# Cross-attention denominators from sums over four steps, joined by an accumulating DMA, in the first batch of a decoder layer

## What is computed

```python
q = (x1 @ wq.T).reshape(b, n, 16, 32).transpose(0, 2, 1, 3)
k = (x2 @ wk.T).reshape(b, m, 16, 32).transpose(0, 2, 1, 3)
v = (x2 @ wv.T).reshape(b, m, 16, 32).transpose(0, 2, 1, 3)
dots = einsum('bhnd,bhmd->bhnm', q, k) * 32 ** -0.5
attn = softmax(dots, axis=-1)
out = einsum('bhnm,bhmd->bhnd', attn, v)       # then @ wo.T + bo, added to x1, layer norm
```

## Time and profile before

| | before |
|---|---|
| three runs | 2017.34, 2019.51, 2024.68 us |
| the profiled execution | 2017.9 us |
| its span, first to last instruction | 2016.1 us |
| PE busy | 1919.1 us (95%) |
| DVE, ACT, POOL busy | 1221.2, 882.5, 793.8 us |
| mean granted TensorE clock | 0.982 of full speed |
| DMA | 211.04 MB moved, 105 GB/s over the span |

### The profile page before, as it was taken

How to read it: one execution, slowest core, us unless ns; L and a number is a source line. 1 busy time by engine, 2 the same in 40 slices (tenths; PEclk the granted TensorE clock), 3 DMA queues, 4 the chain that set the end, 5 groups by cost and what they waited for, 6 DMA issues and landing times.

```text
span 2016.1 us, 26457 instructions
## 1 busy us (share of the span) xinstructions
PE 1919.1 (95%) x10152; PEld 1268.9 (63%) x10152; DVE 1221.2 (61%) x2279; ACT 882.5 (44%) x1587; POOL 793.8 (39%) x705
## 2 busy tenths in 40 slices
PE   6999999989999999999999999999969999999992
PEld 5876665667655555555444545544438999888991
DVE  5565543237677777777778779768654444444433
ACT  3212322222365666666556556546724443333431
POOL 3002200000177777777667657656012222322112
PEclk9999999999999999999999999999979999999996
DMA  6102433574533031312425334422234454444316
GB/s 247 42 1 99 155 107 131 184 220 126 161 96 85 17 76 47 95 43 59 100 65 131 75 93 113 121 48 74 79 111 137 126 138 125 112 136 101 104 22 187
DMA packets 119070, 211.04 MB, mean 105 GB/s; under 512 B 10608, under 2 KB 28672, under 8 KB 118864
## 3 DMA queue, kind: packets, MB, share of 16 engines
q1 hardware_dynamic: 108416, 185.39, 31.2%
q0 software_dynamic: 9440, 21.86, 5.6%
q10 hardware_dynamic: 1088, 2.10, 0.3%
HBM read 147.15 MB, written 62.42 MB: 104 GB/s over the span
## 4 chain that ended last, share of the span: by engine, by line
PE 85%; DVE 10%; DMA 2%; ACT 1%; issue 1%; SPq 0%; POOL 0%; ACTq 0%; POOLq 0%; DVEq 0%
PE banks L1070 36%; PE banks L1236 11%; PE banks L1325 11%; PE banks L1206 10%; PE banks L1225 9%; DVE max L1499 7%; PE banks L1254 5%; PE banks L1076 2%; DMA k_parts<-out_lo 1%; DMA wv_raw<-in_wv_t 1%; DVE stats_y L1707 0%; PE banks L1144 0%; DVE src_lo L1369 0%; DVE wq_lo L1375 0%; ACT src_hi L1754 0%
## 5 line engine op out<-in xcount | busy, mean ns | idle before, releaser
L1499 DVE TENSOR_REDUCE max<-banks 128x1 f32<-128x512 f32 x1024 | 627.6, 683 | 163.3 <-PE banks L1206 162.3
L1969 POOL TENSOR_TENSOR probs_sum<-probs_sum,probs_add 128x512 f32<-128x512 f32 x464 | 581.9, 1285 | 299.8 <-PE banks L1236 299.8
L1206 PE MATMUL banks<-k_stack,q_stack 98*128 98x512 f32 x1024 | 427.8, 425 | 3.7 <-DVE max L1499 2.7
L1847 ACT ACTIVATE probs_sum<-banks 128x512 f32<-128x512 f32 x512 | 264.6, 604 | 296.6 <-PE banks L1225 296.1
L1225 PE MATMUL banks<-q_stack,k_stack 98*128 98x512 f32 x1024 | 377.0, 398 | 2.0 <-ACT probs_sum L1847 2.0
L1206 PEld LDWEIGHTS banks<-k_stack,q_stack 98*128 98x128 f32 x1024 | 192.1, 188 | 190.8 <-issue 82.7
L1847 ACT ACTIVATE probs_add<-banks 128x512 f32<-128x512 f32 x512 | 272.6, 613 | 0.0
L1225 PEld LDWEIGHTS banks<-q_stack,k_stack 98*128 98x128 f32 x1024 | 191.9, 188 | 61.8 <-ACT probs_sum L1847 10.3
L2011 POOL DMA_INDIRECT y_rows<-eo,tok x40 | 81.5, 2037 | 216.4 <-DVE eo L1700 168.9
L1236 PE MATMUL banks<-probs_sum,v_grp 128*32 128x512 f32 x1024 | 139.9, 607 | 0.0
L1687 DVE TENSOR_TENSOR hid_lo<-hid,hid_hi 128x640 fp32r<-128x640 f32 x64 | 52.8, 826 | 140.6 <-ACT hid_hi L1912 140.6
(11 more groups left out here) (233 smaller groups left out, 2785.2 us busy)
## 6 DMA issues: line engine op xcount, KB each, us to landing
k_stack<-k_parts SPq DMA_DIRECT2D x144, 256.0 KB, 4.8
w_raw<-in_L_ffn_w SPq DMA_DIRECT2D x16, 2048.0 KB, 9.7
q_stack<-q_parts SPq DMA_DIRECT2D x48, 256.0 KB
v_grp<-v_rows SPq DMA_DIRECT2D x48, 256.0 KB, 3.1
raw<-in_ctx_t SPq DMA_DIRECT2D x8, 1024.0 KB, 6.7
k_parts<-out_hi SPq DMA_DIRECT2D x32, 256.0 KB, 2.5
k_parts<-out_lo SPq DMA_DIRECT2D x32, 256.0 KB, 2.9
v_rows<-pre SPq DMA_DIRECT2D x32, 256.0 KB, 2.3
```

What stands on the lines that cost most here:

```text
L1206: nc.tensor.matmul(out, queries_of(t)[:, j, tile_of(k)], keys_of(t)[0:STK + SHIFT, j, mc * HALF:(mc + 1) * HALF], start=True, stop=True) \
L1499: V.reduce_max(max4[:, tiles_of(t), :, :][:, k, j, mc:mc + 1], bank(bank_of["max", t, mc, k, j]), AX.X) \
L1847: S.activation(probs_of(t, s)[:, j, :], bank(bank_of["score", t, s, j]), ACT.Exp, scale=SCALE) \
L1969: done = G.tensor_tensor(a[:, j, :], a[:, j, :], b[:, j, :], ALU.add)
```

## The change

In turns 0 to 7, except the last four steps of turn 7, four steps share one denominator (`by_fours`): 31 fours. Their even steps no longer share one set of tiles: step 0 of a four writes `probs_sum` (three tiles, round again after twelve steps), step 2 writes a new set `probs_mid` (two tiles, eight steps), the odd steps write `probs_add` as before. POOL adds both pairs as before, and then issues one DMA that accumulates the tile of `probs_mid` (128 x 2048, 1 MB) into that of `probs_sum`, from SBUF to SBUF (`add_four`). It stands on POOL just ahead of the next pair's addition. The denominator of the four is put in the list three blocks after the four's second pair instead of one. ACT waits for the DMA before it writes the `probs_mid` tile again. The second batch keeps pairs, but its even steps use the two sets too.

The memory for this comes from `y_nat`, now one tile instead of two (the second half's rows are fetched only when the first half's are stored), from moving `earlier`, `kv`, `kv_part` and `att_t`, and from a `dynamic_dma_scratch_size` of 8192. `num_c` gets two buffers, and the inversions of a turn start at another block. The three pieces of a key chunk and the four of a query stack become single entries of the list: in the first batch one of each kind per block, in the second three key pieces.

```diff
+        def by_fours(t, s):
+            return t * MT + s < B * NG * MT - FOUR
+
+        def four_of(t, s):
+            return (t * MT + s) // FOUR % len(probs[0])
...
-                if s == 1:
+                if s == (3 if by_fours(t, 0) else 1):
                     take_bank(("den", t), DEN)
                 do("den", t, s)
                 if s == MT - 1:
                     do("copy_den", t)
                     divisions.extend((t, q) for q in range(PIECES))
+                    divisions_from[0] = clock
...
         def loads_after_scores(t, s):
             stay = stay_of[t]
-            if t == last_of[stay] and s % HT == HT - 1:
-                load_k(stay + 2, s // HT)
-            if s == MT - 1:
-                load_q(t + PLACES)
+            if t == last_of[stay] and s % HT == HT - 1 and stay + 2 < len(stays):
+                key_loads.extend((stay + 2, s // HT, i) for i in range(PARTS))
+            for _ in range(1 if t < B * NG else PARTS):
+                if key_loads:
+                    do("load_k", *key_loads.pop(0))
+            if s == MT - 1 and t + PLACES < len(turns):
+                query_loads.extend((t + PLACES, i) for i in range(PARTS + 1))
+            if query_loads:
+                do("load_q", *query_loads.pop(0))
...
                 if not end:
+                    while fours:
+                        do("add_four", *fours.pop())
                     do("add_pair", turn, s + 1)
-                    pending.append((clock + 1, turn, s + 1))
-                invert(4 if turn == LAST else (0, 2, 2)[s // 2] if s < 6 else 1, 1)
-                if g == NG - 2 and s == 2:
+                    if not by_fours(turn, s):
+                        pending.append((clock + 1, turn, s + 1))
+                    elif s % FOUR == 2:
+                        fours.append((turn, s + 1))
+                        pending.append((clock + 3, turn, s + 1))
+                invert(4 if turn == LAST else 0 if clock == divisions_from[0] else
+                       2 if clock < divisions_from[0] + 3 or turn == B * NG - 1 else 1, 1)
+                if g == NG - 2 and s == 2 and (b or not h):
                     start_side(fetch_rows(b, h))
...
+            place, every = PLACE_OF[s % FOUR]
+            return probs[place][(t * MT + s) // every % len(probs[place])]
...
                     act.wait_ge(*num_summed[t0, s0])
-                    if s0 % 2 == 0:
-                        act.wait_ge(*den_summed[t0, s0 + 1])
+                    if s0 % FOUR == 0:
+                        act.wait_ge(*den_summed[t0, s0 + (3 if by_fours(t0, s0) else 1)])
+                    elif s0 % FOUR == 2:
+                        act.wait_ge(*fours_added[four_of(t0, s0)][t0, s0 + 1] if by_fours(t0, s0)
+                                    else den_summed[t0, s0 + 1])
...
+            def add_four(t, s):
+                pool.wait_ge(*pair_added[t, s])
+                G.dma_start(probs_of(t, s - 3)[:, :, :], probs_of(t, s - 1)[:, :, :], accum_op=ALU.add) \
+                    .then_inc(fours_added[four_of(t, s)].sem, 16)
```

More of the change, by code:

```diff
@@ L182, in program @@
         v_grp = put("v_grp", [P, MT, P])
-        probs = [[put(f"probs_{name}{i}", [P, HG, HALF]) for i in range(n)] for name, n in (("sum", 3), ("add", 3))]
+        probs = [[put(f"probs_{name}{i}", [P, HG, HALF]) for i in range(n)]
+                 for name, n in (("sum", 3), ("add", 3), ("mid", 2))]
         shift_rows = put("shift_rows", [SHIFT * HG * HT, P], F32R)
-        context_base = put.at = put.at + 1024
+        context_base = put.at
         q_stack.append(put("q_stack2", [P, HG, HALF], F32R))
@@ L192, in program @@
         xwo = put("xwo_t", [P, NC, D])
-        y_nat = [put(f"y_nat{i}", [P, HT, D]) for i in range(NH)]
+        y_nat = put("y_nat", [P, HT, D])
         log_parts_at = put.at
@@ L196, in program @@
         hot_col = put("hot_col", [P, TOPK, HT, 2, COLS])
-        num_c = put("num_c", [P, HALF])
+        num_c = [put(f"num_c{i}", [P, HALF]) for i in range(2)]
         den_c = put("den_c", [P, HALF])
@@ L239, in program @@
         bq_col = put("bq_col", [P, NG])
+        kv, kv_part = put("kv", [P, NG, P + HG]), put("kv_part", [P, NG, P + 1])
+        att_t = put("att_t", [P, NG, P])
         den = put("den", [P, H])
@@ L637, in load_k @@
             if stay < len(stays):
-                do("load_k", stay, c)
+                for i in range(PARTS):
+                    do("load_k", stay, c, i)
         def load_q(t):
             if t < len(turns):
-                do("load_q", t)
+                for i in range(PARTS + 1):
+                    do("load_q", t, i)
         def load_v(stay, c):
@@ L742, in side @@
             return True
-        divisions, pending, later = [], [], []
+        divisions, pending, later, fours, divisions_from = [], [], [], [], [0]
         clock = 0
@@ L754, in divide @@
                 elif g == NG - 1 and t < LAST:
+                    if not b and h:
+                        start_side(fetch_rows(b, h))
                     start_side(rows_of(b, h))
@@ L1052, in probs_before @@
         def probs_before(t, s):
-            earlier_step = t * MT + s - 2 * len(probs[s % 2])
+            place, every = PLACE_OF[s % FOUR]
+            earlier_step = t * MT + s - every * len(probs[place])
             return divmod(earlier_step, MT) if earlier_step >= 0 else None
@@ L1157, in fold @@
                 pe.wait_ge(*const_in[()])
-                by_column_groups(out, [(router_pad[:, c, :], y_nat[0][:, c, :]) for c in range(NC)]) \
+                by_column_groups(out, [(router_pad[:, c, :], y_nat[:, c, :]) for c in range(NC)]) \
                     .then_inc(folds_summed.sem, 1)
@@ L1241, in denominators_of @@
             def denominators_of(t, s):
-                if s == 1:
+                first = s - 3 if by_fours(t, s) else s - 1
+                if first == 0:
                     free_bank("den", t)
-                tiles = [probs_of(t, s - 1)]
+                tiles = [probs_of(t, first)]
                 if t == LAST and s == MT - 1:
@@ L1254, in denominators_of @@
                         done = nc.tensor.matmul(bank(DEN)[j * DH:(j + 1) * DH, :], ones[:, 0:DH], tile[:, j, :],
-                                                start=s == 1, stop=s == MT - 1 and tile is tiles[-1])
+                                                start=first == 0, stop=s == MT - 1 and tile is tiles[-1])
                 done.then_inc(den_summed.sem, 1)
@@ L1260, in rows_first @@
                 pe.wait_ge(*xo_added[b, h, k, EARLY])
-                accumulate(out, [(identity[:, :], y_nat[h][:, k, :])], stop=False)
+                accumulate(out, [(identity[:, :], y_nat[:, k, :])], stop=False)
             def rows(b, h, k, part):
@@ L1541, in rows @@
             def rows(b, h, k, part):
-                row = y_nat[h][:, k, :]
+                row = y_nat[:, k, :]
                 dve.wait_ge(*xo_summed[b, h, k, part])
@@ L2179, in fetch_rows @@
             def fetch_rows(b, h):
-                if b:
-                    sp.wait_ge(*x2_out[h][b - 1, h])
-                elif not h:
+                if h:
+                    sp.wait_ge(*x2_out[h - 1][b, h - 1])
+                elif b:
+                    sp.wait_ge(*x2_out[NH - 1][b - 1, NH - 1])
+                else:
                     sp.wait_ge(*folds_summed[()])
                 first = (b * NT + h * HT) * P
-                Q.dma_start(y_nat[h][:, :, :], x1_rows[first:first + HT * P, :].rearrange("(n p) d -> p n d", p=P)) \
+                Q.dma_start(y_nat[:, :, :], x1_rows[first:first + HT * P, :].rearrange("(n p) d -> p n d", p=P)) \
                     .then_inc(y_in[h].sem, 16)
```

80 lines of the change are left out of this document (41 added, 39 removed).

## The result

| | before | after |
|---|---|---|
| median | 2019.77 us (12 runs, 2017.34 to 2024.68) | 2031.4 us (12 runs, 2025.81 to 2038.62) |
| the profiled execution | 2017.9 us, span 2016.1 | 2038.62 us, span 2036.8 |

The ratio is 1.0057, with a 95% interval of 1.0043 to 1.0070. The prediction said 2000 us, 1992 to 2023, and gave "slower" 0.16. It was wrong in its sign and its range. The execution that was profiled after the change is the slowest of its twelve, 7.2 us above the median, so the profile shows somewhat more loss than the medians do.

The account below looks back on a forecast made before the run. PE was taken to bound the kernel, busy 95% of the span. Against the profiled 2017.9 us, -26.7 (matmuls) + 3 (DMA waits) + 4.6 (key piece) = -19.1 gave 1998.8; the median lies 1.6 higher, so 2000 us, range 1992 to 2023.

Parts of the forecast that it names:

- slower: The outcome of a kernel slower than before, given to rival 1 (a slow accumulate); chance 0.16.
- What leaves PE: First batch: two sets of denominator matmuls per four steps become one, 31 times 0.86 us, 26.7 us less.
- The cover: First batch: DVE, ACT and POOL keep up with shorter blocks; POOL has 11.6 us of work in 12.76 per four.
- The room of 9.3 us: From the accumulating DMA's issue to landing, it may take 9.3 us before ACT's next write of the `probs_mid` tile waits.
- L taken as 8.5: L, the accumulating DMA's time from issue to landing: 5.8 us at the best slices' 180 GB/s plus 2.7.
- upper end by engine time: Upper end for the accumulating DMA's landing: four times a 256 KB accumulate's engine time, 8.3, plus 2.7, so 11.0 us.
- Other loads hold the engines 27% of the time: Loads beside the accumulating DMA: some take 10.1 us and cost 0.4; 0.1 on average, 3 us more over 31.
- The key piece: End of turn 7: PE waits for chunk 1's third key piece, issued behind the shift's load; 4.6 us more, once.
- At no cost: Later inversions, second `num_c`, one `y_nat`, and turns 8 to 15 with their pairs add nothing; the experts are unchanged.
- Rival 1: ACT waits on a slow accumulate in block C+3 (C does the four's second pair); slower from L = 10.7 us; chance 0.16.
- Rival 2: Most gain lost: L about 10.3, or POOL's issue 2 us or more; about 2015 us, idle before scores some 17; chance 0.13.
- Rival 3: DVE's inversion holds up POOL's DMA by 0.55 us each; 8.5 us more, about 2008; chance 0.05.

Follow-up runs that it names:

- e1_no_join: The changed kernel without the accumulating DMA and the waits on it, each four's denominator taken from its first pair alone; 2002.88 us.
- e9: Changed kernel, loads issued behind each add of four after its landing, queries first; turn 7 keys three per block; first fours of turns 0, 4 as pairs; 2002.29 us.
- e2_pairs: The changed kernel with pairs in the first batch too, no fours and no accumulating DMA, everything else kept; 2025.35 us.
- e12_pairs_moved: e9 with pairs for all four steps: no accumulating DMA, the loads at e9's places; 2016.48 us.
- e10: e9 without SP's waits for the accumulate's landing, the loads at the same places; 2028.27 us.
- e11: The changed kernel with turn 7's key pieces three per block and the first fours of turns 0 and 4 as pairs, other loads untouched; 2024.81 us.

## Why the prediction was wrong, by its own steps

- **What leaves PE, 26.7 us**: right. 248 fewer matmuls; a turn takes 51.45 us in e1_no_join against 54.88 before, so 3.43 less, and 4 x 0.86 is 3.44; and e1's span by the prediction's terms, 2016.1 - 26.7 + 4.6 + 6 of clock = 2000.0, against 2001.3.
- **The cover**: right. DVE, ACT and POOL held; POOL's issue took 0.84 to 0.95 us (estimate 1.1), and POOL was busy 88% in e9 with PE at 99.8%.
- **The room of 9.3 us**: right, by the timeline of the stall.
- **L taken as 8.5**: this was meant for a DMA without company, and alone it is 6.9 to 7.1. That the median of all, 8.3, is so near is chance: it lies between those and the ones beside loads, 10.3 to 12.9. My upper end by engine time, 11.0, was too long, since a 1 MB accumulate holds the engines for 5.2 us and not for 8.3. The Trainium skill's fit (DMA: Bandwidth & Descriptors, the section on the SWDGE path) gave an estimate of 4.4 us; the trace's quickest landing is 6.9.
- **"Other loads hold the engines 27% of the time, up to 1.6 us more ... I put down 0.1 on average, 3 us more over 31"**: this is the step that failed. A mean share was spread over all DMAs, but the loads come in groups at the end of each turn. In the DMA shown above 4.9 us of engine time fell on one of them; the landings of such became 10.3 to 12.9. Only the excess over 9.3 counts, and that doesn't average out: 16 to 17 us instead of 3. Nor is it shared as (L - 9.3) / 2: a late DMA stands alone between timely ones, and PE pays all of it.
- **A stall priced at its own length**: the second omission, in no term and no rival. The clock cost some 19 us by the ledger, of which e1 has 6 without the DMA.
- **The key piece, 4.6 us once**: right in place and size, 4.52 us at 982.70. With what followed, turn 7 took 58.36 us in e1 against 51.45.
- **At no cost**: right for the second batch (497.3 against 497.1 us). The remainder, by e2_pairs, is little beyond turns 7 and 8.
- **Rival 1** had the place (ACT's wait on the DMA in block C+3) and the sign, but as a slow L in each of the 31; eight were enough. **Rival 2**'s mark, over 15 us idle before the scores, was met (19.3), by a few late landings and not by an L of 10.3 in each four. **Rival 3**: POOL's issue kept to 0.84 to 0.95 us; no sign of a hold by DVE.

## What to carry over

When an edit adds a transfer with a fixed room until someone needs it, don't add the mean traffic to its duration: lay its window over the list of the other queues' issues, and count the ones whose window is full. Charge each excess in full, and on TensorE allow for a half-clock stretch behind it as well. And if the traffic can move, the cheap mend is one wait on the issuing queue, with the pieces that are needed first put first.

## Not expected of the hardware

- **Clock behind short stalls.** 1.7 us idle at 729.29 was followed by a window at 0.76. It can also fall without a stall. In e1_no_join and e9, not before, matmuls of 8 columns that fold the router's weights, in a block without a denominator, were followed by half clock. The missing denominator doesn't explain it alone: in e2_pairs that block has one, and the window 612 to 618 is at 0.73, while in e12_pairs_moved it has one too and the window 612 to 620 is at 1.00. What decides stays open. e1's windows 605 to 610 and 610 to 615:

```profile
605.00:610.00 5.00, 4.90 (x33) 4.02 (x35) 2.66 (x7) 1.74 (x4) 1.34 (x2) 0.83 0.30 74
610.00:615.00 5.00, 5.00 (x25) 1.03 (x18) 0.00 (x0) 0.10 (x1) 3.41 (x3) 0.50 0.00 0
```

- **An accumulating SBUF-to-SBUF DMA of 1 MB** takes 6.9 to 7.1 us alone, and 5.2 of them are engine time; the plain 1 MB store took 4.4 in all.
- **POOL's additions just behind its own DMA issue** are listed longer, 5.28 us for four instead of 5.03, but aren't slower. The first is listed from 704.97 on, and the issue ends at 704.33 + 0.87 = 705.20: the records overlap by 0.23, and the last addition ends 5.05 us behind the issue. The lines are from e9:

```profile
699.00 5.04 POOL L2031 TENSOR_TENSOR probs_mid<-probs_mid,probs_add 128x512 f32<-128x512 f32 x4 [0.84 <-PE banks L1291]
704.33 0.87 POOL L2036 DMA_DIRECT2D probs_sum<-probs_mid  x1 [0.30 <-POOL probs_mid L2031]
704.97 5.28 POOL L2031 TENSOR_TENSOR probs_sum<-probs_sum,probs_add 128x512 f32<-128x512 f32 x4
```

What stays open: 2 to 3 us of e10 and e11 that nothing above holds; why the first scores start up to 6 us apart in runs with the same code ahead of them; and why the low clock differs between stalls of like length.
